# Another order of stages and loads in a two-layer gated cross-attention kernel

## The reference

```python
x = x + tanh(g_xattn[0]) * matmul(fake_quant(layernorm(x)), fake_quant(ctx))
x = x + tanh(g_ffn[0])   * (layernorm(x) @ W_base.T + b_base + 0.5 * transform of low-rank adapters)
x = x + tanh(g_xattn[1]) * attention(layernorm(x), ctx, ctx, mask) @ w_out.T   # 32 heads of 16, 8 key/value groups
x = x + tanh(g_ffn[1])   * bitlinear(relu2(bitlinear(h, w_gate)) * bitlinear(h, w_up), w_down)  # h = layernorm(x)
```

## Time and profile before

| | us |
|---|---|
| median of 3 runs | 252.97 (252.89 to 254.46) |
| the profiled execution | 254.72 |
| its span | 252.9 |

### The profile page before, as it was taken

How to read it: one execution, slowest core, us unless ns; L and a number is a source line. 1 busy time by engine, 2 the same in 40 slices (tenths; PEclk the granted TensorE clock), 3 DMA queues, 4 the chain that set the end, 5 groups by cost and what they waited for, 6 DMA issues and landing times.

```text
span 252.9 us, 4671 instructions
## 1 busy us (share of the span) xinstructions
PE 237.6 (94%) x1450; PEld 122.2 (48%) x1472; DVE 206.9 (82%) x592; ACT 187.4 (74%) x317; POOL 123.2 (49%) x177
## 2 busy tenths in 40 slices
PE   8686999999999999999999999999999999998984
PEld 8522449857543353565354375335335245443532
DVE  1788858588996696897989866989799878899995
ACT  2364696897898999685977988669789989445632
POOL 7004864634350037584786374548998786300000
PEclk9889799999999999999999999999999999999999
DMA  5999961674862930001891000900000000000004
GB/s 174 355 386 441 389 260 35 139 164 117 348 170 66 155 145 3 1 1 45 145 392 64 4 0 21 166 3 1 4 1 0 3 0 0 3 1 0 0 3 166
DMA packets 9154, 27.63 MB, mean 109 GB/s; under 512 B 1514, under 2 KB 4122, under 8 KB 7882
## 3 DMA queue, kind: packets, MB, share of 16 engines
q1 hardware_dynamic: 8698, 21.63, 29.3%
q0 software_dynamic: 288, 5.70, 5.9%
q10 hardware_dynamic: 144, 0.00, 0.0%
HBM read 23.87 MB, written 3.41 MB: 108 GB/s over the span
## 4 chain that ended last, share of the span: by engine, by line
PE 59%; DVE 14%; ACT 9%; issue 7%; POOL 4%; DMA 3%; SPq 2%; DVEq 0%; ACTq 0%; POOLq 0%
PE bank L837 10%; PE bank L809 9%; PE bank L786 8%; PE bank L812 4%; PE bank L718 4%; PE bank L860 4%; PE bank L728 4%; ACT big L1032 3%; DMA big<-in_ctx 3%; PE bank L878 3%; POOL big L594 3%; PE bank L676 2%; PE bank L897 2%; PE bank L795 2%; DVE junk L1259 1%
## 5 line engine op out<-in xcount | busy, mean ns | idle before, releaser
L1259 DVE CUSTOM_DVE_ANT_0 junk<-bank,maskb 128x512 bf16<-128x512 f32 x128 | 82.8, 686 | 12.9 <-PE bank L786 12.4
L1032 ACT ACTIVATE big<-bank 128x512 f32<-128x512 f32 x128 | 73.9, 596 | 17.2 <-PE bank L809 11.2
L594 POOL TENSOR_TENSOR big<-big,product 128x512 int32<-128x512 int32 x48 | 61.6, 1285 | 33.0 <-ACT big L1032 32.6
L809 PE MATMUL bank<-qst,kst 99*128 99x512 bf16 x128 | 48.8, 382 | 0.5
L786 PE MATMUL bank<-kst,qst 96*128 96x512 bf16 x128 | 48.3, 382 | 0.7 <-DVE mx L1259 0.4
L837 PE MATMUL bank<-big,vp 128*32 128x512 f32 x256 | 30.6, 598 | 1.0 <-POOL big L594 0.4
L604 POOL TENSOR_TENSOR mx<-mx 128x4 f32<-128x4 f32 x64 | 14.2, 223 | 23.5 <-DVE mx L1259 21.3
L812 PE MATMUL bank<-ident_b,maskb 128*128 128x512 bf16 x65 | 24.7, 380 | 0.0
L786 PEld LDWEIGHTS bank<-kst,qst 96*128 96x128 bf16 x128 | 12.7, 99 | 22.0 <-issue 10.8
L809 PEld LDWEIGHTS bank<-qst,kst 99*128 99x128 bf16 x128 | 12.4, 97 | 19.1 <-ACT big L1032 9.3
L638 POOL TENSOR_SCALAR stage_w<-stage_w,wscale 128x1376 f32<-128x1376 f32 (+1 forms) x12 | 18.4, 1542 | 5.3 <-DVE wscale L1381 5.3
(11 more groups left out here) (191 smaller groups left out, 412.5 us busy)
## 6 DMA issues: line engine op xcount, KB each, us to landing
stage_w<-in_w_down POOLq DMA_DIRECT2D x1, 2816.0 KB, 9.8
stage_w<-in_w_gate SPq DMA_DIRECT2D x1, 2752.0 KB, 15.2
stage_w<-in_w_up POOLq DMA_DIRECT2D x1, 2752.0 KB, 11.1
qst<-q_parts SPq DMA_DIRECT2D x18, 128.0 KB, 4.9
big<-in_ctxT SPq DMA_DIRECT2D x8, 256.0 KB, 15.3
q_parts<-parts SPq DMA_DIRECT2D x12, 128.0 KB
x<-in_x SPq DMA_DIRECT2D x4, 256.0 KB, 6.3
big<-in_ctx SPq DMA_DIRECT2D x4, 256.0 KB, 6.7
```

The costliest lines, as they stand in the source:

```text
L594: nc.gpsimd.tensor_tensor(p, p, keep[:, nt, KEEP_ST.index(i):KEEP_ST.index(i) + 1, :].broadcast_to([P, HG, P]), ALU.mult).then_inc(kept, 1)
L809: i = mm(o[:, :], kst[0:KM, b, g, s * P:(s + 1) * P], qst[0:KM, tile % 2, g * HG:(g + 1) * HG, :], start=True, stop=by_keep(c, s))
L1032: fn(pt[:, c % 4, s, :], o[:, :], ACT.Exp).then_inc(drain(stage), 1)
L1259: v.tensor_tensor_reduce(junk[:, j % 2, :], o[:, :], maskb[:, tb(c // NG)[1], :], 1.0, HIDE, ALU.add, ALU.max, mx_parts[:, c % 3, 0, hh:hh ...
```

## The change

Only the two lists change. `PREPARATION` has its stages in another order and hands some stages to `FILL` or takes some from it; `FILL` puts stages behind other steps. Both lists together hold the same 852 stages with the fixed pattern, so each engine issues the same instructions in another order. On TensorE the first six stages stay (three `warm`, `k 1 0`, `k 1 1`, `q1T 0`); then `csum 0` comes before `r 0`, and `k 0 1`, `k 1 2` and `we` before `q1T 1`, `v 0 0` before `y0 0 3`. SP's queue begins `wkv, x 0, adapters, ctx 2, 0, 1, x 3, 1, ctxT 5, ctx 3, ctxT 4` instead of `wkv, x 0, 1, ctx 0, 2, 1, ctxT 5, 4, ctx 3`. On VectorE and GpSimd `fscale 0`, and with it the roundings `fround 0`, comes behind `ksplit 0`. In `FILL` the `fabs 2` quarters stand at 75, 82 and 90, `fq 0` at 124 and 126. VectorE's order from `y1up 3` to the end is the same.

```diff
--- before.py
+++ after.py
@@ -74,81 +74,77 @@
 LAG_PV = 25
 
 PREPARATION = [
-    ("load_wkv",), ("vones",), ("scalars",), ("load_x", 0), ("products",), ("xstats", 0), ("ln0", 0, 1),
-    ("ln0", 0, 2), ("load_x", 1), ("ln0", 0, 3), ("ln0", 0, 4), ("ln0", 0, 5), ("load_ctx", 0), ("warm", 0, 0, 42),
-    ("load_ctx", 2), ("warm", 0, 1, 60), ("warm", 0, 4, 10), ("load_ctx", 1), ("xstats", 1), ("cquant", 0),
-    ("ln0q", 0), ("xstats", 2), ("xstats", 3), ("ln0", 1, 1), ("load_ctxT", 5), ("load_ctxT", 4), ("adapters",),
-    ("load_ctx", 3), ("pick",), ("ln0", 1, 2), ("ln0", 1, 3), ("ln0", 1, 4), ("k", 1, 0), ("k", 1, 1), ("load_enc",),
-    ("q1T", 0), ("r", 0), ("ln0", 1, 5), ("csum", 0), ("load_x", 3), ("p", 0), ("load_x", 2), ("ln0q", 1),
-    ("load_adapters",), ("vt",), ("ln0r", 1), ("load_dft", 0), ("k", 0, 0), ("load_dft", 1), ("ln1", 0, 0),
-    ("ln1", 0, 1), ("load_ctxT", 0), ("ln1", 0, 2), ("ln1", 0, 3), ("ln0", 2, 5), ("ln1", 0, 4), ("q1T", 1), ("we",),
-    ("ln1", 0, 5), ("bias", 0), ("hT", 0, 1), ("mask",), ("load_wT", 1), ("load_wT", 3), ("r", 1), ("ln0q", 2),
-    ("p", 1), ("fabs", 0, 0), ("ln0r", 2), ("load_mask",), ("fabs", 0, 1), ("y0up", 0), ("ln2", 0, 0), ("ln2", 0, 1),
-    ("ln2", 0, 2), ("y0", 0, 0), ("y0", 0, 1), ("load_wT", 2), ("ln2", 0, 3), ("ln2", 0, 4), ("ln2", 0, 5),
-    ("ln1", 1, 0), ("y0", 0, 2), ("y0", 0, 3), ("ln1", 1, 1), ("load_bias",), ("k", 0, 1), ("k", 1, 2), ("k", 0, 2),
-    ("k", 0, 3), ("load_wT", 0), ("fsum", 0), ("load_gate",), ("load_ctxT", 1), ("load_ctxT", 6), ("load_ctxT", 2),
-    ("ln1", 1, 2), ("load_ctxT", 3), ("ln1", 1, 3), ("load_ctxT", 7), ("fabs", 0, 2), ("k", 1, 3), ("fabs", 0, 3),
-    ("hT", 0, 2), ("v", 0, 0), ("load_ctx", 4), ("ln1", 1, 4), ("fscale", 0), ("load_wq",), ("v", 0, 1),
-    ("load_ones",), ("v", 0, 2), ("v", 1, 0), ("v", 0, 3), ("q", 0, 0), ("q", 0, 1), ("q", 0, 2), ("q", 0, 3),
-    ("fround", 0, 0), ("fround", 0, 1), ("ksplit", 0), ("ln0", 3, 5), ("cquant", 1), ("ln1", 1, 5), ("bias", 1),
-    ("hT", 1, 1), ("v", 1, 1), ("qsplit", 0), ("fround", 0, 2), ("fround", 0, 3), ("fclamp", 0, 0), ("fclamp", 0, 1),
-    ("fclamp", 0, 2), ("y0", 1, 0), ("y0", 1, 1), ("y0", 1, 2), ("y0", 1, 3), ("fternary", 0, 0), ("y0up", 1),
-    ("vcopy", 0), ("ln2", 1, 0), ("ln2", 1, 1), ("ln0q", 3), ("qpick", 0, 0), ("qpick", 0, 1), ("q1T", 2),
-    ("csum", 1), ("ln2", 1, 2), ("ln2", 1, 3),
+    ("load_wkv",), ("warm", 0, 0, 42), ("warm", 0, 1, 60), ("warm", 0, 4, 10), ("load_x", 0), ("scalars",),
+    ("products",), ("load_adapters",), ("xstats", 0), ("ln0", 0, 1), ("ln0", 0, 2), ("ln0", 0, 3), ("k", 1, 0),
+    ("load_ctx", 2), ("adapters",), ("k", 1, 1), ("ln0", 0, 4), ("ln0", 0, 5), ("xstats", 1), ("load_ctx", 0),
+    ("load_ctx", 1), ("cquant", 0), ("load_x", 3), ("load_x", 1), ("load_ctxT", 5), ("load_ctx", 3), ("load_ctxT", 4),
+    ("vones",), ("q1T", 0), ("ln0q", 0), ("csum", 0), ("xstats", 2), ("xstats", 3), ("ln0", 1, 1), ("ln0", 1, 2),
+    ("load_x", 2), ("load_dft", 1), ("r", 0), ("load_dft", 0), ("load_ctxT", 0), ("pick",), ("ln0", 1, 3),
+    ("ln0", 1, 4), ("p", 0), ("ln1", 0, 0), ("load_ctxT", 1), ("ln1", 0, 1), ("vt",), ("load_wT", 2), ("load_wT", 1),
+    ("ln0", 1, 5), ("ln0q", 1), ("load_enc",), ("ln1", 0, 2), ("ln1", 0, 3), ("ln1", 0, 4), ("load_ctxT", 6),
+    ("k", 0, 0), ("k", 0, 1), ("load_bias",), ("ln0r", 1), ("k", 1, 2), ("load_wT", 0), ("load_mask",), ("we",),
+    ("q1T", 1), ("ln1", 0, 5), ("hT", 0, 1), ("bias", 0), ("load_gate",), ("r", 1), ("load_wT", 3), ("ln0q", 2),
+    ("p", 1), ("fabs", 0, 0), ("fabs", 0, 1), ("fclamp", 0, 0), ("y0", 0, 0), ("ln0", 2, 5), ("y0", 0, 1), ("mask",),
+    ("y0", 0, 2), ("load_ctxT", 2), ("load_ctxT", 3), ("ln0r", 2), ("v", 0, 0), ("fabs", 0, 2), ("fabs", 0, 3),
+    ("fround", 0, 0), ("y0", 0, 3), ("q1T", 2), ("load_ctxT", 7), ("load_ones",), ("load_wq",), ("y0up", 0),
+    ("ln2", 0, 0), ("ln2", 0, 1), ("ln2", 0, 2), ("ln2", 0, 3), ("ln2", 0, 4), ("fsum", 0), ("load_ctx", 4),
+    ("k", 0, 2), ("ln2", 0, 5), ("k", 0, 3), ("k", 1, 3), ("v", 0, 1), ("v", 0, 2), ("ksplit", 0), ("fscale", 0),
+    ("hT", 0, 2), ("v", 1, 0), ("v", 0, 3), ("ln1", 1, 0), ("q", 0, 0), ("q", 0, 1), ("q", 0, 2), ("ln1", 1, 1),
+    ("ln1", 1, 2), ("q", 0, 3), ("cquant", 1), ("ln1", 1, 3), ("ln1", 1, 4), ("ln1", 1, 5), ("bias", 1),
+    ("fround", 0, 1), ("r", 2), ("hT", 1, 1), ("ln0q", 3), ("ln0", 3, 5), ("qsplit", 0), ("csum", 1), ("y0", 1, 0),
+    ("fround", 0, 2), ("vcopy", 0), ("y0up", 1), ("ln2", 1, 0), ("fclamp", 0, 1), ("y0", 1, 1), ("ln2", 1, 1),
+    ("y0", 1, 2), ("y0", 1, 3), ("qpick", 0, 0), ("load_wo",), ("qpick", 0, 1),
 ]
 
 FILL = {
-    0: [("ln2", 1, 4)], 1: [("v", 1, 2), ("ln2", 1, 5)], 2: [("fternary", 0, 1)],
...
-    6: [("q", 1, 0)], 7: [("ksplit", 1), ("fclamp", 0, 3), ("q", 1, 1), ("p", 2)], 9: [("vcopy", 1)],
...
-    22: [("hT", 2, 1), ("fclamp", 1, 0)], 24: [("qsplit", 1)], 25: [("fabs", 1, 0)],
-    26: [("y0", 2, 0), ("y0", 2, 1), ("y0", 2, 2), ("y0", 2, 3), ("fclamp", 1, 1), ("fabs", 1, 1), ("fabs", 1, 2)],
...
-    30: [("p", 3), ("oT", 0)], 34: [("aT", 0, 0), ("fscale", 1)], 38: [("keepT",), ("fround", 1, 0)],
...
-    44: [("fclamp", 1, 2), ("hT", 2, 2)], 46: [("fround", 1, 3), ("q", 2, 0), ("oT", 1)], 48: [("aT", 0, 1)],
...
-    74: [("ln2", 3, 0), ("ln2", 3, 1), ("ln2", 3, 2), ("ln2", 3, 3), ("ln2", 3, 4), ("fabs", 2, 0), ("fabs", 2, 1),
-        ("fabs", 2, 2), ("ln2", 3, 5)],
...
-    104: [("fround", 2, 0), ("fround", 2, 1), ("hidden", 0, 0)],
-    105: [("fround", 2, 2), ("fround", 2, 3), ("ln3", 1, 5), ("ln3", 1, 6), ("fclamp", 2, 1)],
...
-    120: [("hidden", 0, 2), ("fq", 0, 0)], 121: [("fclamp", 2, 2), ("fclamp", 2, 3), ("fternary", 2, 1)],
-    123: [("fq", 0, 1)], 124: [("fternary", 2, 2), ("fternary", 2, 3)], 126: [("y1", 2, 1)],
-    127: [("fq", 0, 2), ("f1T", 1)], 128: [("y1", 2, 2)], 130: [("gu", 1, 0, 0), ("gu", 1, 0, 1)],
-    131: [("fq", 0, 3)], 132: [("gu", 1, 1, 0), ("y1", 2, 3), ("hidden", 1, 0), ("y1up", 2)], 133: [("ln3", 2, 0)],
...
+    0: [("v", 1, 1), ("fternary", 0, 0), ("fternary", 0, 1), ("ln2", 1, 2)],
...
+    10: [("fternary", 0, 2), ("fternary", 0, 3), ("fclamp", 0, 2), ("fclamp", 0, 3), ("q", 1, 1), ("q", 1, 2),
...
+    24: [("y0", 2, 0), ("y0", 2, 1), ("y0", 2, 2), ("y0", 2, 3), ("qsplit", 1), ("y0up", 2), ("ln2", 2, 0),
+        ("ln2", 2, 1), ("ln2", 2, 2), ("fabs", 1, 0), ("fabs", 1, 1), ("ln2", 2, 3)],
...
+    36: [("fround", 1, 0), ("ln1", 3, 0)], 38: [("oT", 0)], 39: [("ln1", 3, 1), ("fround", 1, 1), ("ln1", 3, 2)],
+    40: [("fround", 1, 2), ("fternary", 1, 0)], 41: [("fclamp", 1, 2)], 42: [("fround", 1, 3)],
...
+    75: [("fabs", 2, 0)], 76: [("hT", 3, 2)], 77: [("ln3", 0, 5)], 78: [("q", 3, 0), ("oT", 3)],
+    81: [("ln3", 0, 6), ("q", 3, 1)], 82: [("fabs", 2, 1), ("q", 3, 2), ("q", 3, 3)], 83: [("f1T", 0)],
...
+    88: [("gu", 0, 0, 0), ("ln3", 1, 0)], 89: [("ln3", 1, 1)], 90: [("ln3", 1, 2), ("fabs", 2, 2), ("fabs", 2, 3)],
+    94: [("ln3", 1, 3), ("gu", 0, 0, 1), ("fsum", 2)], 95: [("fscale", 2)], 98: [("oT", 4)], 103: [("aT", 2, 0)],
+    105: [("fround", 2, 0)], 106: [("fround", 2, 1), ("hidden", 0, 0), ("ln3", 1, 4), ("ln3", 1, 5)],
+    107: [("fround", 2, 2), ("fternary", 2, 0)], 110: [("gu", 0, 1, 0), ("ln3", 1, 6)], 111: [("gu", 0, 1, 1)],
+    112: [("hidden", 0, 1), ("fround", 2, 3), ("fclamp", 1, 3), ("gu", 0, 2, 0), ("oT", 5)], 114: [("gu", 0, 2, 1)],
...
+    123: [("ffactors", 0)], 124: [("fq", 0, 0), ("fq", 0, 1), ("fq", 0, 2)], 126: [("fq", 0, 3), ("y1", 2, 1)],
...
 }
```

11 lines of the change are left out of this document (5 added, 6 removed), and 60 rows, old and new, of the table FILL.

## The result

The changed kernel takes 250.30 us (median of 4 runs, 249.81 to 251.41), the kernel before 253.31 in the 4 runs beside it: ratio 0.987, 95% interval 0.983 to 0.991, so 3 us less where 1.2 was forecast. The profiled execution took 250.55 us around a span of 248.7, against 254.72 around 252.9.

A forecast was written before the change was run, and what follows sets the result against it. TensorE, busy 237.6 of 252.9 us, was taken as the bound, with VectorE pacing the last part. Terms +2.5 + 0.4 - 0.7 - 2.2 - 1.7 + 0.9 - 0.4 = -1.2 us gave 251.8, range 250.4 to 253.0 (outer 249.2 to 254.6).

The forecast's parts named there:

- First hole: TensorE's early wait for context slice 4: more loads ahead start `k 1 0` +2.5 us later, bounds +2.0 and +3.5.
- rival B: Slower: loads ahead of slice 4 make it land near 16.0 and lengthen the early wait; 254.3 us, chance 0.10.
- +0.4 for a low clock that reaches further: Low clock after TensorE's first long wait may reach into the products behind: +0.4 us, 0 to +0.9.
- `r 0` and the second hole: Prologue: `csum 0` covers the wait of `r 0`, -0.7 us; moved products fill the wait before the second q1T, -2.2.
- The second low clock: Low clock from 25.0 to 28.5 goes with the wait before it: half of 3.5 us of work, -1.7.
- New waits: Rest of the prologue: TensorE may newly wait at three places, 0 to 2.1 us, taken as +0.9.
- The split beside the roundings: VectorE's last split step, 1.12 us beside GpSimd's roundings, becomes near 0.7; frees some 2 us, counted as nothing.
- Rival A: VectorE sets the prologue's pace: first score drained 2.3 us earlier, -2.9 us in all, 250.0; chance 0.22.
- The long middle: From 60 to 225 us, spread sums and roundings of `w` 2 gain -0.4 us, at most the idle 2.6.
- `fq 0` ahead of the scores' end: `fq 0 2` and `fq 0 3` move ahead of the last score, loading VectorE: up to +2.4 us, taken as nothing.
- Rival C: VectorE is late at the end of the scores and the 2.4 us are all paid: 254.2 us, chance 0.08.
- The tail: Behind `y1up 3`, VectorE's part with unchanged stage order: 27.8 us carried over whole.

The follow-up runs named there:

- e3: Changed kernel with the new order only up to step 11 and the old order from step 12 on: 253.35 us, ratio 1.000.
- e8: Changed kernel with context slices 5 and 4 and `ctx 3` ahead of the adapters and `x` 3, 2 in SP's queue: 250.61 us, ratio 0.988.
- e4: Changed kernel with `we` behind `q1T 1` and `k 0 1`, `k 1 2` back in front of `k 0 2`: 254.58 us, ratio 1.000.
- e10: Kernel before with only weight 2's absolute sums and roundings and `fq 0` parts 2, 3 at their new steps: 254.76 us, ratio 1.006.
- e1: Changed kernel with the old order of all stages behind step 69: 252.22 us, ratio 0.997.
- e2: Kernel before with the new order behind step 69 alone: 251.20 us, ratio 0.992.
- e7: Changed kernel with VectorE's `fq 0` parts 1, 2, 3 put later, at steps 126, 127, 131: 252.21 us, ratio 0.993.
- e5: Changed kernel with GpSimd's four roundings of weight 2 back at steps 104 and 105: 252.67 us, ratio 0.996.
- e6: Changed kernel with ScalarE's absolute sums of weight 2 back at steps 74 and 82: 251.47 us, ratio 0.991.
- e9: e8 with `wT` 3 and context slices 2 and 3 also ahead of the gate weights in SP's queue: 254.12 us, ratio 1.001.

## Why the prediction was right, and where it was not

The time, 250.3, is 1.5 us below the forecast of 251.8. It lies inside the outer range of 249.2 to 254.6 but just below the forecast's own, 250.4 to 253.0; I had given 0.27 to a time below 250.4. The direction is in large part luck: the prologue, in which I saw two thirds of the gain, is worth nothing clear by itself (e3, ratio 1.000), and nearly all of the 3 us lie where I saw 0.4.

- **First hole.** Forecast +2.5, measured +3.2 (14.82 against 11.60): slice 4, issued at 6.20, landed near 14.7, near the 15.1 from which I had set rival B. Mis-sized within its bounds. What failed is the premise that this hole has a price: e8 takes 2.85 us of it away, and the first score (one execution) and the ratio (0.988) stay. Nothing is left of the +0.4 for a low clock that reaches further; the products took 3.40 us and what followed ran at full speed.
- **`r 0` and the second hole.** Right against the profile that I read: both waits are gone (-0.7, -2.2), and e4, with the hole restored, has its first score 2.3 us later. In the execution that e10 shows only 0.55 us of the second hole are there to be gained.
- **The second low clock, -1.7.** Right for the profiled execution of before, wrong for its median: by their mean clock 26 of 35 runs don't have it. I had written that the profiled execution stood 1.75 us above the median and then subtracted that difference from both sides, when it was the very term. For the median run the sum should have been -1.2 + 1.7 = +0.5, which is 253.5, a kernel that gains nothing, and e3, which is the prologue and the first steps alone, measured about that (253.35, ratio 1.000).
- **New waits, +0.9.** The largest is 0.5 us; TensorE idles 0.42 us from 29.3 to 54.8 instead of 0.05. So +0.4 or more. The 31.9 us for slice 3 doesn't come out of my own rate: 9996 KB stand in the queue up to and with it, 6880 behind slice 4, which at 0.71 us per 256 KB and 14.1 for slice 4 makes 33.2; it landed at 33.7. TensorE came there later too, so the miss cost almost nothing. Nor does 52.8 for the first score come out of my terms: 54.80 - 0.8 for the prologue - 0.9 for the `v` product owed is 53.1. It measured 52.48, and the spread of 51.59 to 53.46 holds both.
- **The split beside the roundings.** 0.69 us instead of 1.12, as said; no run takes its worth apart. Rival A forecast 250.0 and the time is 250.3, but not by its mechanism: VectorE takes the first score 0.65 us behind TensorE instead of 0.94, 0.3 us, and the prologue alone (e3) does not make the time.
- **The long middle, -0.4.** This is the step that failed. From the first score to `y1up 3` I had the lead fall from 2.0 to 1.2 us; it rose from 2.3 to 4.2. I had bounded the gain by the idle time of 2.6 us and taken a seventh of it. Behind step 69 alone M falls by 2.17 (e1) or 1.95 us (e2). The bound was wrong in kind too: within M TensorE idles 0.83 us in e1 and 1.26 in the changed kernel, which is 2.17 us faster. "Busy" is no measure of density, since a product of 0.38 us is followed by the next 0.22 us later when nothing waits. In the kernel before:

```profile
187.80 0.39 PE L809 MATMUL bank<-qst,kst 99*128 99x512 bf16 x1
188.02 0.38 PE L786 MATMUL bank<-kst,qst 96*128 96x512 bf16 x1
188.42 0.39 PE L809 MATMUL bank<-qst,kst 99*128 99x512 bf16 x1
188.65 0.38 PE L812 MATMUL bank<-ident_b,maskb 128*128 128x512 bf16 x1
```

  The third starts 0.40 us after the second, where the same pair of lines is 0.22 or 0.23 apart in 56 of 64 cases within M. These 0.18 us are a wait, and they count as busy.
- **`fq 0` ahead of the scores' end, 0 to +2.4, taken as 0.** Wrong sign on the new order: undoing it costs 0.94 us (e7). Rival C (254.2) had it backwards, since it counted the work that moves ahead and not whom it meets.
- **The roundings and absolute sums of weight 2.** I named them and gave them a third of an idle time. On the new order they are worth 1.14 and 0.72 us (e5, e6).
- **The tail.** 27.83 forecast, 27.86 measured.

Two errors partly cancel: 1.7 us counted that the median run did not have, some 2 us behind step 69 and up to 1 us in steps 12 to 69 not counted. What stays open is why the rest of the new order behind step 69 alone costs 0.63 us. The gain of steps 12 to 69 wasn't taken apart either (e1 lies 1.1 us below e3 in the medians, 0.6 at a mean clock of 0.991 or more).

## What to carry to other kernels

Before a term is taken from a profiled execution that stands above the median, ask whether the term is the difference: here a second stretch of low clock stood in the profile and, by the mean clocks, in about one run of four. In a kernel with in-order queues, don't price a moved stage by its length and by idle time, but by what it now stands in front of and beside: here the same three moves save 2.8 us on one order of the other stages and cost 1.1 us on the other. And a distance between two instructions inside the full-clock part repeated to 0.03 us here, far better than a median of runs, so measure single edits there; laying the two timelines product by product on each other then names the place of the loss.

## What the runs showed of the hardware

- The same kernel has its low clock in different places from run to run, and for 3.4 or for 6.8 us: 14.3 to 17.7 in one execution of the changed kernel, 11.2 to 18.0 in another; e8 has runs with a mean clock of 1.000. After waits of TensorE of nearly the same length the clock fell or did not: it fell, within 1.3 us of the work's return, behind 2.25 us (before), 2.19 (e8) and 3.44 (e9), and stayed full behind 2.69 (e9) and 3.10 (e4). The two profiles with a second hole near 24 and a mean clock of 0.986 or 0.987 (before and e2) have a second low stretch behind it, and 9 of 35 runs of the kernel before list that mean clock; e4 lists 0.971 to 0.986 in 7 of 12.
- Closing the first hole to 2.2 us came with a mean clock of 1.000 in three of six runs and left the time where it was (ratio 0.988 both times), as transfers paced that part.
- VectorE's rounding of 128 x 352 took 0.34 us alone and 1.45 beside GpSimd's multiply; an operation of VectorE on 128 x 1 took 0.19 alone and 0.95 beside one.
